# Graph kernel, one core: edge counts by blocks of five destinations with fetched edges of their own

## What is computed

```
counts[d, s] = number of edges s -> d, plus 1 on the diagonal for d < 625   # uint16, read by the third graph layer's attention
sums[d, s]   = sum of edge_weight over the edges s -> d                      # float32
agg = sums @ x                # segment_sum(edge_weight * x[src], dst): layers 2 and 4
```

## Time and profile before

| what | value |
|---|---|
| median of 3 runs | 5692.63 us (5689.88 to 5702.6) |
| profiled execution, its own time | 5696.73 us |
| its span | 5695.1 us |
| TensorE busy over the span | 4594.2 us (81%) |
| VectorE busy | 2710.8 us (48%) |
| ScalarE busy | 2078.4 us (36%) |
| GpSimd busy | 863.2 us (15%) |
| mean granted TensorE clock | 0.892 |

### The profile page before, as it was taken

One profiled execution on the slowest core, in us unless ns is written; L12 is line 12 of the kernel. 1 busy time (PEld: TensorE's weight loads), 2 busy tenths in 40 slices (PEclk: granted clock), 3 DMA queues, 4 the chain that ended last, 5 costly groups with the idle time before them and its releaser, 6 DMA issues. The chain is left out here.

```text
span 5695.1 us, 88397 instructions
## 1 busy us (share of the span) xinstructions
PE 4594.2 (81%) x24482; PEld 3867.0 (68%) x24483; DVE 2710.8 (48%) x5117; ACT 2078.4 (36%) x3240; POOL 863.2 (15%) x789
## 2 busy tenths in 40 slices
PE   3788868888865499778689989989759959989766
PEld 2677745555544399548578878778649959979755
DVE  5455567777754400221279779779741131020233
ACT  2333314544442210323256556556524321020232
POOL 2777710000004300002100000000012210000000
PEclk8788879999977799889899999999869979999978
DMA  3433312111122433104211111111022133324100
GB/s 95 115 110 111 99 34 77 71 76 71 76 67 89 119 135 139 31 17 132 66 50 57 38 50 57 43 45 59 26 85 68 65 84 146 144 77 157 59 17 24
DMA packets 150164, 438.51 MB, mean 77 GB/s; under 512 B 25592, under 2 KB 89805, under 8 KB 133676
## 3 DMA queue, kind: packets, MB, share of 16 engines
q1 hardware_dynamic: 115212, 341.23, 16.9%
q0 software_dynamic: 34848, 96.08, 6.0%
HBM read 340.98 MB, written 96.25 MB: 77 GB/s over the span
## 5 line engine op out<-in xcount | busy, mean ns | idle before, releaser
L2448 PE MATMUL p_acc<-p_H,p_eT 125*125 125x256 f32 x3750 | 823.5, 378 | 0.0
L2448 PEld LDWEIGHTS p_acc<-p_H,p_eT 125*125 125x125 f32 x3750 | 695.2, 187 | 106.0
L1033 POOL DMA_INDIRECT p_message<-edge_table,p_index x425 | 502.8, 1183 | 132.2 <-issue 119.7
L1934 DVE BATCH_NORM_STATS2 features_stats<-F x60 | 29.2, 486 | 888.8 <-ACT F L1925 887.3
L1246 PE MATMUL p_acc<-p_message,p_spread 125*125 125x260 f32 x1666 | 423.3, 421 | 28.6 <-issue 28.6
L1705 ACT ACTIVATE p_hid<-p_up,p_b1s 128x125 f32<-128x125 f32 x764 | 272.3, 365 | 397.4 <-PE p_up L1681 353.9
L1246 PEld LDWEIGHTS p_acc<-p_message,p_spread 125*125 125x125 f32 x1666 | 346.8, 210 | 97.3 <-issue 30.5
L1681 PEld LDWEIGHTS p_up<-p_xT,p_w1s 128*128 128x128 f32 x3056 | 377.1, 199 | 51.3 <-issue 33.8
L1681 PE MATMUL p_up<-p_xT,p_w1s 128*128 128x125 f32 x3056 | 384.8, 283 | 32.7 <-issue 12.4
L835 PE MATMUL p_acc<-p_cell,p_heavy 125*125 (+1 forms) x1440 | 401.4, 389 | 0.0
L1298 POOL IOTA p_order_i<- 125x200 int32 x3 | 1.1, 381 | 2441.9 <-SPq L81 2441.9
(11 more groups left out here) (462 smaller groups left out, 8054.7 us busy)
## 6 DMA issues: line engine op xcount, KB each, us to landing
sums_first<-edge_sums SPq DMA_DIRECT2D x48, 1250.0 KB
p_second<-edge_sums SPq DMA_DIRECT2D x48, 1250.0 KB, 7.4
p_count<-edge_counts SPq DMA_DIRECT2D x75, 762.9 KB
edge_sums<-p_sums SPq DMA_DIRECT2D x32, 1250.0 KB
edge_counts<-p_total SPq DMA_DIRECT2D x32, 610.4 KB
p_w1s<-in_L_ffn_W SPq DMA_DIRECT2D x16, 1024.0 KB
p_got<-made SPq DMA_DIRECT2D x25, 560.0 KB
p_dst_all<-dst_row SPq DMA_DIRECT2D x25, 531.2 KB, 3.9
```

What stands on the lines that cost most here:

```text
L1033: pool.indirect_dma_start(message[:, m, k, :], None, table, bass.IndirectOffsetOnAxis(ap=index[:, m, k:k + 1], axis=0)).then_inc(landed[m] ...
L2448: last = pe.matmul(acc[:, s, 0:C], eT[:, r % 4, a % 4], H[:, a, 0:C], start=(a == 0), stop=(a == T - 1))
```

## The change

The blocks become 640 of five destinations. The host lays dst, src and weight of the edges out as rows of four int32 (`edges`), and each block gets the 128 edges from its first one on, loaded by SP during the attention into partitions (`own_edges`, which lies in `XT`). An edge of a later block makes a `cell` outside the 125 columns and so counts nothing there. `load_graph` now finds, for each block, the number of edges below it: six indirect loads fetch the chunk in which it begins, and VectorE counts in it. `count_edges` visits each block once, in 160 batches of four: VectorE makes `low` and `cell` as float32, 4 x 125 columns each; GpSimd makes `heavy` as `low` times the weight; TensorE makes one float32 product for the counts (`cell` on the left, so that no transpose is wanted) and one for the sums; ScalarE copies out both. The counts lie with destination and tile on 125 partitions, and a group's store has pieces of 125 uint16. Blocks of over 128 edges get the rest in a loop behind the stores, which runs at least once.

```diff
-BLK = 20
-TB = 5
-GD = TB * BLK
+BLK = 5
+EB = 128
+KB = 4
+BG = 20
+GD = BG * BLK
 GROUPS = -(-N // GD)
-BLOCKS = GROUPS * TB
-FIRSTS = 512
+BLOCKS = GROUPS * BG
+BATCHES = BLOCKS // KB
+LOADS = 26
+STARTS = 6 * P
+FAR = 1 << 20
...
+            pool.wait_ge(reached, 1)
+            for m in range(6):
+                pool.indirect_dma_start(found[:, m].rearrange("p e k -> p (e k)"), None, edges.rearrange("(c e) k -> c (e k)", e=P),
+                                        bass.IndirectOffsetOnAxis(ap=row[:, m:m + 1], axis=0)).then_inc(found_loaded, 16)
...
+            for m in range(6):
+                then(dve.tensor_scalar(below[:], ends_all[:, 0], start[:, m:m + 1], None, ALU.is_lt))
+                then(dve.tensor_tensor_reduce(out=scratch[:], in0=below[:], in1=rank[:], scale=1.0,
+                                              scalar=0.0, op0=ALU.mult, op1=ALU.max, accum_out=reach[:, m:m + 1]))
+            dve.tensor_copy(row[0:P], reach[:]).then_inc(reached, 1)
...
-            n = BLOCKS
...
-            prefix(n, before[:])
...
+            dve.wait_ge(found_loaded, 96)
+            then(dve.tensor_copy(value[:], found[0:P, :, :, 0]))
+            then(dve.tensor_tensor(value[:], value[:], start[:].unsqueeze(2).to_broadcast([P, 6, P]), ALU.is_lt))
+            then(dve.tensor_reduce(begin[:], value[:], AX_X, ALU.add))
+            dve.scalar_tensor_tensor(out=begin[:], in0=reach[:], scalar=float(P), in1=begin[:], op0=ALU.mult, op1=ALU.add).then_inc(begin_ready, 1)
...
+            then(dve.tensor_copy(g.begins[:].rearrange("p (a b) -> p a b", a=2), turned[:, :, 0:3 * P]))
+            then(dve.tensor_copy(g.starts[:], g.begins[:]))
...
+def begin_rest(dve, then, g, over, over_i, total):
+    then(dve.tensor_scalar(g.next_edge[:], g.begins[:, 0:BLOCKS], float(EB), None, ALU.add))
+    then(dve.tensor_tensor(g.rest_edges[:], g.begins[:, 1:BLOCKS + 1], g.next_edge[:], ALU.subtract))
+    then(dve.tensor_scalar(over[:], g.rest_edges[:], float(EB - 1), 0.0, ALU.add, ALU.max))
+    then(dve.tensor_copy(over_i[:], over[:]))
+    then(dve.tensor_scalar(over_i[:], over_i[:], 7, None, ALU.arith_shift_right))
+    then(dve.tensor_copy(over[:], over_i[:]))
+    then(dve.tensor_reduce(total[:], over[:], AX_X, ALU.add))
+    then(dve.tensor_scalar(total[:], total[:], 1.0, None, ALU.max))
+    then(dve.tensor_copy(g.pick_i[:, 1:2], total[:]))
+    then(dve.tensor_copy(g.next_edge_i[:], g.next_edge[:]))
+def pick_rest(dve, then, g, over):
+    then(dve.tensor_scalar(over[:], g.number[:], -1.0, float(BLOCKS), ALU.mult, ALU.add))
+    then(dve.scalar_tensor_tensor(out=over[:], in0=g.rest_edges[:], scalar=0.0, in1=over[:], op0=ALU.is_gt, op1=ALU.mult))
+    then(dve.tensor_reduce(g.pick[:, 0:1], over[:], AX_X, ALU.max))
+    then(dve.tensor_scalar(g.pick[:, 0:1], g.pick[:, 0:1], -1.0, float(BLOCKS), ALU.mult, ALU.add))
+    then(dve.tensor_scalar(g.pick[:, 0:1], g.pick[:, 0:1], float(BLOCKS - 1), None, ALU.min))
+    then(dve.tensor_copy(g.pick_i[:, 0:1], g.pick[:, 0:1]))
+def count_edges(nc, g, edges, own, counts, weights):
...
+            pool.memset(sums[96:128].rearrange("p a h d -> p (a h d)"), 0.0).then_inc(cleared, 1)
...
+            def one(n, k, i):
+                at = k % SLOTS
+                pool.wait_ge(low_ready, n + 1)
+                pool.tensor_tensor(heavy[:, at], low[:, at], own[:, bass.ds(n * KB, KB), 2:3].bitcast(F32).to_broadcast([EB, KB, P]),
+                                   ALU.mult).then_inc(heavy_ready, 1)
...
+            lanes = lane[:].unsqueeze(1).to_broadcast([EB, KB, P])
+            def one(n, k, i):
+                def each(of):
+                    return of[:, bass.ds(n * KB, KB)].unsqueeze(2).to_broadcast([EB, KB, P])
+                at = k % SLOTS
+                dve.wait_ge(batch_used, n + 1)
+                dve.tensor_tensor(low[:, at], lanes, each(lo), ALU.is_equal).then_inc(low_ready, 1)
+                dve.tensor_tensor(cell[:, at], lanes, each(key), ALU.is_equal).then_inc(cell_ready, 1)
+            over_batches(dve, one)
...
+            rests = rest_total(dve)
+            with dve.Fori(0, rests) as v:
...
+                dve.tensor_tensor(rest_heavy[:], rest_low[:], rest[:, 2:3].bitcast(F32).to_broadcast([EB, P]), ALU.mult).then_inc(rest_made, 1)
...
+                then(dve.tensor_tensor(old_counts[:], old_counts[:], acc[0:P, 0, 0, 0:P], ALU.add))
+                then(dve.tensor_tensor(old_sums[:], old_sums[:], acc[0:P, 0, 1, 0:P].rearrange("p (d h) -> p h d", h=T), ALU.add))
...
+            def one(n, k, i, looped=False):
+                at = k % SLOTS
+                pe.wait_ge(batch_kept, n + 1)
+                pe.wait_ge(low_ready, n + 1)
+                pe.wait_ge(cell_ready, n + 1)
+                pe.wait_ge(heavy_ready, n + 1)
+                for q in range(KB):
+                    own_block = n * KB + q if looped else BLOCKS
+                    loops = own_block * BLK < LOOPED
+                    pe.matmul(acc[0:P, at, 0, q * P:(q + 1) * P], cell[:, at, q], low[:, at, q], start=True, stop=not loops, skip_group_check=True)
+                    if loops:
+                        t, first = own_block * BLK // P, own_block * BLK % P
+                        pe.matmul(acc[0:P, at, 0, q * P + first:q * P + first + BLK], g.ident[0:P, 0:P],
+                                  g.ident[0:P, 0:P].rearrange("p (d h) -> p d h", h=T)[:, :, t], start=False, stop=True, skip_group_check=True)
+                    last = pe.matmul(acc[0:P, at, 1, q * P:(q + 1) * P], heavy[:, at, q], cell[:, at, q], start=True, stop=True, skip_group_check=True)
+                last.then_inc(batch_used, 1)
...
+                if s == 0:
+                    turn = i * 2 + k // (2 * (BG // KB))
+                    act.wait_ge(stored[m], turn * 32 + 32)
+                    act.wait_ge(sums_stored[m], turn * 16 + 16)
+                act.wait_ge(batch_used, n + (SLOTS + 1))
+                act.activation(total[:, m, s * KB:(s + 1) * KB].rearrange("p b l -> p (b l)"), acc[0:P, k % BANKS, 0, 0:KB * P], ACT.Copy)
+                act.activation(sums[0:P, m, :, s * KB * BLK:(s + 1) * KB * BLK],
+                               acc[0:P, k % BANKS, 1, 0:KB * P].rearrange("p (b d h) -> p h (b d)", b=KB, h=T), ACT.Copy).then_inc(batch_kept, 1)
...
+            load_rest(picked_block())
             with sp.Fori(0, GROUPS // 2) as i:
                 for m in range(2):
                     j = i * 2 + m
-                    sp.wait_ge(block_kept, j * TB + (TB + 2))
+                    sp.wait_ge(batch_kept, j * (BG // KB) + (BG // KB + BANKS))
                     sp.dma_start(weights[bass.ds(j * ROWS, ROWS), :], sums[:, m].rearrange("p h d -> p (h d)")).then_inc(sums_stored[m], 16)
-                    sp.wait_ge(flip_kept, (j + 1) * len(FLIPS) + 4)
-                    sp.dma_start(counts[bass.ds(j * GD, GD), :], total[:]).then_inc(stored, 16)
+                    split_rows(sp, table[bass.ds(j * BG, BG)].rearrange("b p l -> p b l"), total[:, m], stored[m])
             for m in range(2):
                 sp.wait_ge(sums_stored[m], 8 * GROUPS + 16)
-            sp.wait_ge(stored, 16 * GROUPS + 16)
+                sp.wait_ge(stored[m], 16 * GROUPS + 32)
+            with sp.Fori(0, rests) as v:
+                b = picked_block()
+                old_total = table[tile(b)].rearrange("a p l -> (a p) l")
+                old = columns[bass.ds(group * ROWS, P), :, bass.ds(place * BLK, BLK)]
+                sp.dma_start(old_counts[:], old_total).then_inc(old_loaded, 16)
+                sp.dma_start(old_sums[:], old).then_inc(old_loaded, 16)
+                sp.wait_ge(rest_added, v + 1)
+                sp.dma_start(old_total, old_counts[:]).then_inc(rest_stored, 16)
+                sp.dma_start(old, old_sums[:]).then_inc(rest_stored, 16)
+                sp.wait_ge(rest_stored, v * 32 + 32)
+                sp.wait_ge(picked, v * 6 + 6)
+                sp.nop(nofuse=True)
+                load_rest(picked_block())
+            sp.wait_ge(rest_loaded, rests * 16 + 16)
...
+                for a in range(0, LOADS, LOADS // 2):
+                    b = r * LOADS + a
+                    for k, s in enumerate(g.starts_of(nc, mybir.EngineType.SP, b, LOADS // 2)):
+                        sp.dma_start(own_edges[:, bass.ds(b + k, 1), :].rearrange("p a k -> p (a k)"), edges[bass.ds(s, EB), :]).then_inc(own_edges_loaded, 16)
...
+            rest_then = Steps(dve, rest_setup)
+            begin_rest(dve, rest_then, g, over, over_i, rests)
+            pick_rest(dve, rest_then, g, over)
...
+    edges = np.zeros((E + 3 * P, 4), np.int32)
+    edges[:, 0] = FAR
+    for k, name in enumerate(("dst", "src", "edge_weight")):
+        edges[0:E, k] = a[name].view(np.int32)
+    out["edges"] = edges
...
+                own_edges = XT[:, 0, 0:4 * LOADS * ROUNDS].bitcast(I32).rearrange("p (b k) -> p b k", k=4)
```

(40 more changed lines are left out.)

327 lines of the change are left out of this document (134 added, 193 removed).

## The result

The changed kernel takes 5341.48 us (median of four runs, 5335.57 to 5347.74); the kernel before took 5697.0 beside it. The ratio is 0.9377, with a 95% interval of 0.936 to 0.9394. The forecast was 5345. The total is right, but two terms of its largest part were wrong by some 70 us each, in opposite directions, as the windows by stage show.

The account below looks back on a forecast made before the run. The prediction took the old count stage (853 us) as bound by loaded TensorE and VectorE and the order between them. It summed 5696.7 - 356 (stage) + 8 (attention) - 3 (load_graph) = 5345.7, forecast 5345 us, range 5225 to 5530.

Parts of the forecast that it names:

- Self-loops: Count loop, first 32 batches: 8 more short TensorE instructions each, 10 us added in all (0 if hidden, 31 if not).
- The low clock: Rival for the count loop: TensorE at 1.2 GHz throughout, loop 572 us, total 5491; chance 0.12.
- Turns: Count loop: VectorE's two comparisons and GpSimd's product exclude each other, 1.36 + 1.15, taken as 2.6 us a batch.
- The mixed clock of 0.80: Count loop: TensorE at full clock 0.6 of the time, as in the attention, giving 2.5 us a batch.
- no turns: Rival for the count loop: VectorE and GpSimd don't alternate, TensorE at full clock sets 2.0 us a batch, total 5255; chance 0.18.
- the rest pass: End of the counts: the loop for fuller blocks runs once alone, 30 us of pieces and 15 of waits, 45 us.
- 30 ns a piece: Count stores: price of a 250 B piece, making 7.9 us a group, hidden under 13 us.
- bound of 62 ns: Count stores: price of a piece above which a group's stores are no longer hidden.
- The third rival: Count stores: short pieces cost say 100 ns and bind, 19.1 us a group, total 5634; chance 0.12.
- Drain: End of the count loop: last batch through TensorE and ScalarE, then the last group's stores, 12 us.
- the step "hidden": Attention: SP's 26 added loads a round (13 us of 27) and late destination loads are hidden; cost 8 us (0 to 40).
- all three signs named for a wrong forecast: ScalarE waiting for a store each group; TensorE full at a clock near 0.5; SP's loads showing gaps in attention gathers.

Follow-up runs that it names:

- the first run: The changed kernel as first measured and profiled (also called the first profile), against the kernel before: 5341.48 us, ratio 0.9377.
- x1: Changed kernel with the self-loops' products left out, so those counts are missing from the output: 5232.93 us.
- x9: Changed kernel with each batch's self-loops in one short bf16 product (two where the source block changes) ahead of the long products: 5234.18 us, ratio 0.9183.
- x10: Changed kernel with VectorE writing the cells of a batch first and the low one-hots second: 5325.11 us.
- x4: Changed kernel with counts stored in 5,000 B pieces and no product on GpSimd (sums of weights become counts): 5298.29 us.
- run 60: Not a run: words of the quoted "gathers run 60 us first", the 60 us that the attention's gathers run at its start; no measured time.
- x5: The changed kernel unaltered, run and profiled a second time: 5328.3 us, ratio 0.9348 to the kernel before.

## Why the prediction came out

**Right, by its own working:** the order of the gain, that the set-up takes 15.2 us (14), that GpSimd and VectorE exclude each other for the most part, and that their sum, not TensorE, sets the pace of a batch without self-loops (but for the 0.34 us a group that the stores added in the first run). ScalarE's two evictions take 1.25 us a batch, within the 1.2 to 1.7.

**The total is near by luck.** In the first profile the counts took 19 us less than forecast (478 for 497), the attention ended 13 later (809.1 for 795.9), and the stages behind took 8 more: 2 in all. Inside the counts, larger errors cancel.

**The loop, 422 us for 426, is right by two errors.**

- *Self-loops.* The step that failed is "I add 10 us in all (0 if hidden, 31 if not)". It priced eight short instructions a batch by their length. The first 32 batches took 161 us, where the forecast had 32 x 2.6 + 10 = 93: 68 more. The low clock was a rival for the whole loop (0.12), argued against with "then it is busy all the time, as in the old loop". TensorE was busy all the time, at 0.50, and the router's row of the kernel before (20.7 of 20.7 us, 0.50) already spoke against that argument. x1 and x9 show that the products themselves go with it. That rival put the self-loops at 38 us, which no row gives; 32 x 8 instructions at the 209 ns of the earlier trace rows are 54, and with 32 x 3.34 for the long ones make 161, which is what was measured.
- *Turns.* For 2.6 us a batch the turns take 2.01, and a batch with the stores' share 2.04 in the first profile: 128 x 0.56 = 72 less. The mechanism was right and its terms too large: comparisons follow each other at 0.60, not 0.68; the product alone takes 1.02, not the 1.15 of the earlier trace rows; about 0.2 us overlap. The Trainium skill (SBUF — State Buffer, Who interferes with whom) has a VectorE instruction with two SBUF inputs contend with a GpSimd one that reads SBUF, for a port pair that it calls an exclusive lock. x10 agrees in the main: beside a comparison the product grows from 1.02 to 1.28 us, 0.26 of the 0.40 us that a full exclusion would cost it, and `low` grows from 0.67 to 1.50 beside the product.
- *TensorE.* A batch has 1.745 us at full clock, not 1.92 (an instruction takes 109 ns, not the 120 of the earlier trace rows); of a later batch's 2.04 us that is 86%, not 75 (the profile shows it busy 231.75 of 261.3 us, 89%). The mixed clock of 0.80, carried over from the attention, described neither part: it is 0.50 and then 0.99. The rival "no turns" had the right pace, 2.0, for the wrong reason: in x4, without the product and with long pieces, TensorE's own is 1.745. (That rival also takes 35 us for the rest pass where the forecast takes 45, without saying why.)

**Stores.** 30 ns a piece was low: 38 to 48, 9 to 10.5 us a group. The forecast's bound of 62 ns held only under groups of 13 us; under 10.04 it is (10.04 - 3.06) / 160 = 44 ns, which the first profile passed and the second didn't. The third rival was thus true in part in the first run, for about 9 us. The Trainium skill (DMA: Bandwidth & Descriptors, Specifications) has transfers under 512 B read, modified and written, and gives no price there. The doubling of the 60 ns of the earlier trace rows was the forecast's own supposition: a stored piece of 250 B costs less than that row, so no run here shows a doubling.

**Ends.** Drain 18.8 us for 12: the last group's stores take some 10 us, not 8, and start behind the counts of the group before, whose issue ends only at 1247.8 us (1239.22 + 8.62). The rest pass 22.0 for 45: its 20-byte pieces take (1272.0 - 1266.9) = 5 us to load and some 10 to store, 8 and at most 17 ns at the forecast's 625 an engine, not 24, and the three waits are in those 22.

**The attention, +18 for +8,** within 0 to 40, but the step "hidden", because "gathers run 60 us first", named the wrong user. The late second destination load was wanted at 127 by ScalarE, not by the gathers; its delay of 13 us went through the round's one-hots and TensorE to GpSimd's fifth round (68 gathers are out by then), a stall of 21.2 us at 199.8. The forecast's sign for it, a gap in the gathers, is there once. load_graph gave 0.3 us (it ends at 44.46 for 44.8), not 3.

So all three signs named for a wrong forecast appeared (waits for stores, TensorE full near 0.5, a gap in the gathers), and the total hardly moved, because the turns were shorter by as much. Nothing in the forecast made that likely.

## What to carry to other kernels

A total that comes out right proves none of its terms: check each by its own window. Before adding short products, look in the old trace for a stretch of the same shape and read its granted clock. When work is handed to GpSimd to spare VectorE, price it as a turn on VectorE if both read two tiles; here VectorE alone was faster (1.77 us a batch for 2.01). Before moving small DMAs into another stage's queue, ask which engine's first use stands behind them, and let the first rounds' own loads go ahead.

## What the runs showed of the hardware

- TensorE was shown busy for all of 160.7 us and stayed at a granted clock of 0.50 (1.2 GHz) while a third of its instructions had five columns; with one short product a batch the clock was 1.00 (2.4 GHz) from 835 to 985 us. In the kernel before it was shown busy for 20.7 us on products of eight columns, at 0.50. Here a full busy share didn't go with the upper level.
- The same stores of one kernel took 9.2 us a group in one execution (x5) and 10.5 in another (the first profile), 40 and 48 ns a piece of 250 B.
- SP stood 4.8 to 9.5 us in the issue of 13 rows of counts behind 112 others in the first profile, 4.8 to 6.7 in x5. Loads of 128 pieces of 16 B cost SP 0.68 us each (17.76 / 26), where the earlier trace rows had 0.51.
